# An affine LN with its residual and the plain LN behind it, run as one block chunk by chunk

## The chip, the core and the metric

The kernel runs on one core of a Trainium2 chip. The metric is the time of one execution on the device in microseconds (us): 1481.65 us, the median of three runs (1480.32 to 1482.69).

## The reference

Eight stages A to H work on an activation x of 4 x 1024 tokens by 128 features in float32. Most of them are x + f(LN(x)). The change touches what stands between stage B or D (a feedforward with nine paths, of which each token takes one) and the attention of stage C or E:

```python
def _layernorm(h, gamma, beta):                      # end of the feedforward, EPS = 1e-05
    mu = jnp.mean(h, axis=-1, keepdims=True)
    var = jnp.var(h, axis=-1, keepdims=True)
    return (h - mu) * jax.lax.rsqrt(var + EPS) * gamma + beta
...
    return _layernorm(x + collapsed, gamma, beta)    # added to the residual stream
...
def _layernorm(x, axis=-1, eps=1e-05):               # in front of the next stage, no gain, no bias
    m = jnp.mean(x, axis=axis, keepdims=True)
    v = jnp.var(x, axis=axis, keepdims=True)
    return (x - m) / jnp.sqrt(v + eps)
```

So per place X becomes X + (z - mean) / sqrt(var + eps) * gamma + beta, and Y becomes the plain LN of that new X.

## The kernel before

The activation lies transposed in SBUF: 128 features on the partitions, 4096 tokens (NT) along the free axis. It is worked on in 8 chunks (NCH) of 512 tokens (CH). X is the residual stream, Y what the next stage reads, `k.big[1]` (a part of `arena`) the feedforward's result z. PSUM has eight banks of 128 x 512 float32, `k.bank[0]` to `k.bank[7]`.

The statistics run over the partitions, so TensorE makes them with two constant matrices: `k.center` (identity less 1/128) gives the centered chunk, and `k.mean` (all 1/128) times its squares gives the variance, already spread over all partitions. A float32 matmul of 512 columns shows as two records (and two weight loads) in the trace.

`layernorm` (line 75) is one block: a function for each engine, all of which meet at the block's start and end. It takes the chunks in two loop turns of four (W = 4). For chunk c:
- TensorE (L91) centers it into bank c as soon as `ln_out` says that chunk c - 4 is done, later (L94) makes the variance in bank 4 + c.
- ScalarE squares the centered chunk into `ln_sq` (L103), then makes 1/sqrt(var + eps) as exp(-0.5 ln(var + eps)) in `ln_std`: Ln at L111, Exp at L113.
- VectorE multiplies the two (L122). With gain and bias it applies them in place (L126), and adds the result to X (L130).

Each engine executes its instructions in the order of the code, and each `wait_ge` holds back all that stands behind it on that engine. `ln_out` starts at 4 (`PRIMED`), so that the first four chunks needn't wait.

`stage_ffn` (L806) calls `layernorm` for its input, then `feedforward`, then `layernorm` with gamma, beta and the residual (L811). `stage_favor` and `stage_segments` begin with a block that sets their semaphores (`begin_stage`), then call the plain `layernorm` into Y (L1445, L1785), with the stage's weight loads on SyncE and its small constants on GpSimd in the same block (`favor_loads`, `segment_loads`). After that comes the attention's own block. The stages before and after them, and all other LNs, are the same in both kernels.

Of the kernel before, what the change touches and what calls it, by code (L numbers as in the profile page):

```python
# [6 lines left out]
ALU = mybir.AluOpType  # L7
ACT = mybir.ActivationFunctionType
# [7 lines left out]
CH = 512  # L16
NCH = NT // CH
# [47 lines left out]
def plain(buf, it, c):  # L65

    return buf[:, bass.ds(it * (W * CH) + c * CH, CH)]
# [7 lines left out]
def layernorm(nc, k, call, src, dst, gain=None, bias=None, residual=None, ahead=None):  # L75
# [57 lines left out]
        k.ln_scaled_0 += NCH  # L133
    if residual is not None:
        k.ln_biased_0 += NCH


def rwkv_loads(k, a, block):
# [667 lines left out]
def stage_ffn(nc, k, a, X, Y):  # L806
    call = k.ff_calls
    k.ff_calls += 1
    k.ln(X, lambda it, c: padded(k.N, it, c), ahead=(lambda block: ffn_loads(k, a, block)) if call == 0 else None)
    feedforward(nc, k, a, call)  # L810
    k.ln(lambda it, c: plain(k.big[1], it, c), None, gain="gamma", bias="beta", residual=X)  # L811


def lru(nc, k, a):
# [621 lines left out]
def stage_favor(nc, k, a, X, Y):  # L1436
    with ExitStack() as ctx:
        sems = begin_stage(nc, ctx, FAVOR_SEMS)
        (k.fw_in, k.fw_mask, k.fw_turned, k.fw_wide, k.fw_copied, k.fv_proj, k.fv_sq, k.fv_norm, k.fv_nm, k.fv_v, k.fv_va,
         k.fv_score, k.fv_max, k.fv_off, k.fv_arg, k.fv_exp, k.fv_used, k.fv_ysum, k.fv_acc, k.fv_sums, k.fv_kv,  # L1440
         k.fv_exT, k.fv_ratio, k.fv_ln, k.fv_rd, k.fv_o, k.fv_out, k.fv_x) = sems
        k.ln(X, Y, ahead=lambda block: favor_loads(nc, k, a, block))
        favor(nc, k, a)
        end_stage(nc, sems)

# [334 lines left out]
def stage_segments(nc, k, a, X, Y):  # L1780
    with ExitStack() as ctx:
        sems = begin_stage(nc, ctx, SEGMENT_SEMS)
        (k.sw_in, k.sw_mask, k.sg_proj, k.sg_first, k.sg_kv, k.sg_q, k.sg_kd, k.sg_vd, k.sg_score, k.sg_max, k.sg_arg, k.sg_exp,
         k.sg_sum, k.sg_weight, k.sg_mul, k.sg_turned, k.sg_pT, k.sg_vT, k.sg_vt, k.sg_pv, k.sg_ov, k.sg_out, k.sg_x, k.sg_quarters, k.sg_ln, k.sg_half) = sems
        k.ln(X, Y, ahead=lambda block: segment_loads(nc, k, a, block))  # L1785
        segments(nc, k, a)
        end_stage(nc, sems)

# [1 line left out]

SEMS = ["passed", "ident_zero", "ident_one", "consts_set", "vrows_set", "vecs_in", "vecs_turned", "vecs_ready",
        "x_turned", "x_ready", "x_ready_a", "ln_centered", "ln_squared", "ln_var", "ln_logs", "ln_rstd",
        "ln_scaled", "ln_biased", "ln_out", "y_turned", "y_rows", "y_rows_a", "stored", "wA_in", "moe_w_in", 
        "ff_w_in", "ff_const", "ff_spread", "ff_spread16", "ff_hot0", "ff_mix1", "ff_mix2", "ff_mix", "ff_up",
        "ff_u", "ff_h", "ff_hid", "ff_score", "ff_step", "ff_hot", "ff_hotT", "ff_hot16", "ff_spreads", "ff_masked", "ff_out",
        "ff_z", "lr_w_in", "lr_prod", "lr_read", "lr_init", "lr_sc", "lr_den", "lr_ln", "lr_rden", "lr_step", "lr_x", "lr_kv", "lr_out", "lr_added", "tw_in",
# [13 lines left out]
PRIMED = {"ln_out": 4, "rt_copied": 4,  # L1810
          "ex_r": 4, "ex_relu": 2, "ex_v": 2, "ex_gate": 2, "ex_added": 2, "ex_tanh": 1, "ex_weighed": 1, "ex_sq": 1,
          "ff_h": 6, "ff_out": 1, "ff_hid": 3, "ff_masked": 6, "ff_z": 2, "lr_read": 6, "lr_added": 2,
          "tr_th": 2, "tr_lpT": 1, "tr_x": 2, "tr_z": 2, "tr_g": 1, "tr_turned": 2, "tr_out": 2}
# [122 lines left out]
def build(nc, a, out):  # L1936
    with ExitStack() as ctx:
        def sb(name, shape, dt=F32):
            return ctx.enter_context(nc.sbuf_tensor(name, shape, dt))

        k = Chip()
        k.sems = [ctx.enter_context(nc.semaphore(name)) for name in SEMS]
        (k.passed, k.ident_zero, k.ident_one, k.consts_set, k.vrows_set, k.vecs_in, k.vecs_turned,
         k.vecs_ready, k.x_turned, k.x_ready, k.x_ready_a, k.ln_centered, k.ln_squared, k.ln_var,
         k.ln_logs, k.ln_rstd, k.ln_scaled, k.ln_biased, k.ln_out, k.y_turned, k.y_rows, k.y_rows_a, k.stored, k.wA_in, k.moe_w_in,
         k.ff_w_in, k.ff_const, k.ff_spread, k.ff_spread16, k.ff_hot0, k.ff_mix1,
         k.ff_mix2, k.ff_mix, k.ff_up, k.ff_u, k.ff_h, k.ff_hid, k.ff_score, k.ff_step, k.ff_hot, k.ff_hotT,
         k.ff_hot16, k.ff_spreads, k.ff_masked, k.ff_out, k.ff_z, k.lr_w_in, k.lr_prod, k.lr_read, k.lr_init, k.lr_sc,
# [13 lines left out]
        k.arena = sb("arena", [P, 5 * NT])  # L1962
        k.big = [k.arena[:, i * NT:(i + 1) * NT] for i in range(5)]
        k.rows = k.big[0].rearrange("p (t d) -> p t d", d=P)
        k.ln_calls = k.ff_calls = k.tr_calls = 0

        k.weights = sb("weights", [P, 5120])
        k.eWk = k.weights[:, 0:2048].rearrange("p (e f) -> p e f", e=E)
# [87 lines left out]
```

## Time and profile before

| | us |
|---|---|
| median of three runs | 1481.65 |
| lowest, highest | 1480.32, 1482.69 |
| the profiled execution | 1488.51 |
| its span, first to last instruction | 1486.8 |

The mean granted clock of TensorE in the profiled execution is 0.923 of full speed. All rows come from this one execution; its span is 5 us over the median of the timed runs. Times in the timeline are us from the start of the span. A row of the timeline can merge several instructions of one line; the bracket gives the idle time of the engine before it and what ended it. In the view by stretches the columns are the stretch, its length, the busy us of PE (matmuls), PEld (weight loads), DVE (VectorE), ACT (ScalarE) and POOL (GpSimd) with the count of instructions that start in it, the granted clock of TensorE as a share of full speed, and the DMA share and GB/s.

### The profile page before, as it was taken

What the parts mean: (1) busy time and instruction counts of PE and PEld (TensorE: products, weight loads), DVE (VectorE), ACT (ScalarE), POOL (GpSimd) and SP (SyncE); (2) the same over time, 40 slices, a digit from 0 to 9 for tenths busy, and PEclk for the clock granted to TensorE, in tenths of its full rate; (3) what the DMA queues carried; (4) which work ended last, traced back from release to release, by engine and by line L of the source; (5) the groups of instructions that cost most, each with busy time, mean ns of one, the idle gap of its engine ahead of it and who ended that gap; (6) DMA issues with size and microseconds to landing.
All of it is one profiled execution on the core that took longest, in us unless ns stands there. A gap on an engine that the chain in (4) does not pass through costs nothing. (4 is left out here: it accounts for less than half of the span.)

```text
span 1486.8 us, 22417 instructions
## 1 busy us (share of the span) xinstructions
PE 1226.7 (83%) x7613; PEld 664.2 (45%) x7636; DVE 1006.7 (68%) x1607; ACT 849.1 (57%) x1375; POOL 342.9 (23%) x383
## 2 busy tenths in 40 slices
PE   6888589999999689789997796798898875774656
PEld 3333244444444234257763342376666743431244
DVE  2577458888888355457772555599899945839576
ACT  5677455555555533555675435688877755363442
POOL 0000113333333100000000000187777640005100
PEclk8899889999999889979998999899999998897789
DMA  4000000000000000000000000000000000000001
GB/s 135 1 0 0 0 1 0 0 0 0 0 0 0 9 1 0 8 1 2 2 2 1 0 0 7 1 2 2 2 2 2 3 12 0 0 8 0 0 1 56
DMA packets 9270, 9.77 MB, mean 7 GB/s; under 512 B 2702, under 2 KB 7648, under 8 KB 9184
## 3 DMA queue, kind: packets, MB, share of 16 engines
q1 hardware_dynamic: 9136, 8.61, 1.9%
q8 instruction: 54, 0.88, 0.2%
q14 instruction: 32, 0.26, 0.1%
q10 hardware_dynamic: 48, 0.01, 0.0%
HBM read 6.52 MB, written 2.10 MB: 6 GB/s over the span
## 5 line engine op out<-in xcount | busy, mean ns | idle before, releaser
L575 POOL TENSOR_TENSOR arena<-arena 128x512 f32<-128x512 f32 x64 | 104.7, 1635 | 218.8 <-DVE arena L492 218.8
L556 ACT ACTIVATE arena<-psum 128x512 f32<-128x512 f32 x128 | 69.5, 595 | 127.7 <-PE psum L523 127.7
L523 PE MATMUL psum<-arena,weights 128*128 128x512 f32 x256 | 122.0, 599 | 6.6 <-DVE arena L482 5.9
L538 PE MATMUL psum<-arena,weights 128*128 128x512 f32 x256 | 120.4, 592 | 0.1
L91 PE MATMUL psum<-X,center 128*128 x128 | 75.7, 712 | 35.8 <-PEq L58 16.2
L482 DVE SCALAR_TENSOR_TENSOR arena<-diff,vecs,N 128x512 f32<-128x512 f32 x64 | 102.5, 1602 | 0.0
L122 DVE TENSOR_TENSOR Y<-psum,ln_std 128x512 f32 x48 | 33.2, 692 | 87.9 <-ACT ln_std L113 87.9
L94 PE MATMUL psum<-ln_sq,mean 128*128 128x512 f32 x192 | 91.0, 596 | 0.0
L1656 ACT ACTIVATE N<-N 128x1024 f32<-128x1024 f32 x64 | 67.8, 1059 | 37.5 <-DVE N L1745 36.8
L1562 PE MATMUL psum<-arena 32*128 32x128 f32 x1024 | 79.7, 297 | 4.8 <-ACT arena L1626 4.8
L1572 PE MATMUL psum<-ident,N 128*128 128x128 f32 x512 | 73.2, 288 | 12.3 <-POOL N L1709 11.1
L1562 PEld LDWEIGHTS psum<-arena 32*128 32x128 f32 x1024 | 67.0, 199 | 31.9 <-issue 16.1
L1652 ACT ACTIVATE arena<-psum 128x1024 f32<-128x1024 f32 x64 | 65.5, 1023 | 19.7 <-PE psum L1572 19.5
L489 DVE SCALAR_TENSOR_TENSOR arena<-arena,psum 128x512 f32<-128x512 f32 x64 | 44.0, 687 | 48.3 <-PE psum L538 48.3
L523 PEld LDWEIGHTS psum<-arena,weights 128*128 128x128 f32 x256 | 48.3, 191 | 62.7 <-issue 48.6
L538 PEld LDWEIGHTS psum<-arena,weights 128*128 128x128 f32 x256 | 48.6, 190 | 61.3 <-issue 60.8
L103 ACT ACTIVATE ln_sq<-psum 128x512 f32<-128x512 f32 x96 | 55.0, 589 | 30.0 <-PE psum L91 30.0
L111 ACT ACTIVATE ln_std<-psum,eps 128x512 f32<-128x512 f32 x96 | 64.9, 676 | 7.3 <-PE psum L94 7.3
L563 ACT ACTIVATE arena<-arena 128x1024 f32<-128x1024 f32 x64 | 68.3, 1068 | 0.0
L1709 POOL TENSOR_TENSOR N<-N,arena 128x512 f32<-128x512 f32 x64 | 67.7, 1058 | 0.0
L1708 POOL TENSOR_TENSOR N<-N,arena 128x512 f32<-128x512 f32 x64 | 66.8, 1043 | 2.0 <-ACT arena L1662 2.0
L1572 PEld LDWEIGHTS psum<-ident,N 128*128 128x128 f32 x512 | 57.5, 145 | 21.6 <-POOL N L1709 16.2
(338 smaller groups left out, 2723.8 us busy)
## 6 DMA issues: line engine op xcount, KB each, us to landing
arena<-in_L_attn_a_x_dram SPq DMA_DIRECT2D x4, 512.0 KB, 5.4
out_dram<-arena SPq DMA_DIRECT2D x4, 512.0 KB, 3.3
weights<-in_L_attn_a_eWk_dram SPq DMA_DIRECT2D x1, 1024.0 KB, 5.7
weights<-in_L_attn_a_eWr_dram SPq DMA_DIRECT2D x1, 512.0 KB, 9.4
weights<-in_L_attn_b_W_rkv_dram SPq DMA_DIRECT2D x1, 192.0 KB, 2.3
ffw<-in_L_ffn_W_dram SPq DMA_DIRECT2D x9, 16.0 KB
ffw<-in_L_ffn_W_dram SPq DMA_DIRECT2D x1, 144.0 KB
arena<-n_L_ffn_leaf_values_dram SPq DMA_DIRECT2D x1, 128.0 KB
```

The source lines that it names most:

```text
L91: nc.tensor.matmul(k.bank[c][:], k.center[:], src(it, c), start=True, stop=True).then_inc(k.ln_centered, 1)
L94: nc.tensor.matmul(k.bank[2 + c][:], k.mean[:], k.ln_sq[:, c - 2, :], start=True, stop=True).then_inc(k.ln_var, 1)
L482: nc.vector.scalar_tensor_tensor(mixed[:, j % 4, 1, :], k.diff[:, c, :], k.vec(f"cm_r{e}"), before, ALU.mult, ALU.add).then_inc(k.ex_mix, 1)
L523: op = nc.tensor.matmul(k.bank[2 * (j % 2) + h][:], k.eWk[:, e, h * P:(h + 1) * P], mixed[:, j % 4, 0, :], start=True, stop=True)
L538: op = nc.tensor.matmul(k.bank[4 + j % 2][:], k.eWv[:, e, h, :], ks[:, (2 * (j % 2) + h) * CH:(2 * (j % 2) + h + 1) * CH], start=(h == 0), ...
L556: op = nc.scalar.activation(kr[:, h * CH:(h + 1) * CH], k.bank[2 * (j % 2) + h][:], ACT.Relu)
L563: nc.scalar.activation(ks[:, (j % 2) * 2 * CH:(j % 2 + 1) * 2 * CH], kr, ACT.Square).then_inc(k.ex_sq, 1)
L575: nc.gpsimd.tensor_tensor(acc[:, c, :], acc[:, c, :], oj, ALU.add).then_inc(k.ex_added, 1)
L1562: op = nc.tensor.matmul(scored[half][:, e * P:(e + 1) * P], k.sg_Q[b % 2][at, seg, 2 * j:2 * j + 2, :].rearrange("p h n -> p (h n)"), k.sg ...
L1572: op = nc.tensor.transpose(turned_to[:, e * P:(e + 1) * P], pr[n % 4][:, e * P:(e + 1) * P], k.ident[:])
L1656: nc.scalar.activation(pr[n % 4], pr[n % 4], ACT.Exp).then_inc(k.sg_exp, 1)
L1709: nc.gpsimd.tensor_tensor(others, others, spread(sm[n % 4][:, 8:40]), ALU.mult).then_inc(k.sg_mul, 1)
```

## The change

Both calls, the affine LN at the end of stages B and D and the plain LN at the start of C and E, are replaced by one call of `layernorm_pair` behind `begin_stage`. It takes eight chunks without a loop. Banks 0 and 1 hold the centered chunks of the first LN, 2 and 3 its variances, 4 and 5 the centered chunks of the second, 6 and 7 its variances; the slots of `ln_sq` and `ln_std` are divided in the same way, so that each of these has two places, used by chunks in turn. The first LN has seven semaphores of its own (`lp_...`). In its turn i an engine works on chunk i, i - 1, i - 3 or i - 4, by the step:

```diff
+def layernorm_pair(nc, k, src, gain, bias, dst, ahead):
+
+
+
+    a0, b0 = k.lp_calls * NCH, k.ln_calls * NCH
+    out0 = b0 + PRIMED["ln_out"]
+    first, second = [k.bank[0], k.bank[1]], [k.bank[4], k.bank[5]]
+    first_var, second_var = [k.bank[2], k.bank[3]], [k.bank[6], k.bank[7]]
+    sq = [[k.ln_sq[:, 2 * j + s, :] for s in range(2)] for j in range(2)]
+    std = [[k.ln_std[:, 2 * j + s, :] for s in range(2)] for j in range(2)]
+    scaled = [k.diff[:, s, :] for s in range(2)]
+    at = lambda c: slice(c * CH, (c + 1) * CH)
+    with nc.Block() as block:
+        ahead(block)
+
+        @block.tensor
+        def _(pe):
+            def center(c):
+                if c >= 2:
+                    pe.wait_ge(k.lp_scaled, a0 + c - 1)
+                nc.tensor.matmul(first[c % 2][:], k.center[:], src[:, at(c)], start=True, stop=True).then_inc(k.lp_centered, 1)
+
+            def variance(c):
+                pe.wait_ge(k.lp_squared, a0 + c + 1)
+                if c >= 2:
+                    pe.wait_ge(k.lp_logs, a0 + c - 1)
+                nc.tensor.matmul(first_var[c % 2][:], k.mean[:], sq[0][c % 2], start=True, stop=True).then_inc(k.lp_var, 1)
+
+            def center_again(c):
+                pe.wait_ge(k.lp_out, a0 + c + 1)
+                if c >= 2:
+                    pe.wait_ge(k.ln_out, out0 + c - 1)
+                nc.tensor.matmul(second[c % 2][:], k.center[:], k.X[:, at(c)], start=True, stop=True).then_inc(k.ln_centered, 1)
+
+            def variance_again(c):
+                pe.wait_ge(k.ln_squared, b0 + c + 1)
+                if c >= 2:
+                    pe.wait_ge(k.ln_logs, b0 + c - 1)
+                nc.tensor.matmul(second_var[c % 2][:], k.mean[:], sq[1][c % 2], start=True, stop=True).then_inc(k.ln_var, 1)
+
+            for i in range(NCH + 4):
+                if i < NCH:
+                    center(i)
+                if 0 <= i - 3 < NCH:
+                    center_again(i - 3)
+                if 0 <= i - 1 < NCH:
+                    variance(i - 1)
+                if 0 <= i - 4 < NCH:
+                    variance_again(i - 4)
+
+        @block.scalar
+        def _(act):
+            act.preload_act_table_set("natural_log_exp_and_others")
+
+            def square(c):
+                act.wait_ge(k.lp_centered, a0 + c + 1)
+                if c >= 2:
+                    act.wait_ge(k.lp_var, a0 + c - 1)
+                nc.scalar.activation(sq[0][c % 2], first[c % 2][:], ACT.Square).then_inc(k.lp_squared, 1)
+
+            def over(c):
+                act.wait_ge(k.lp_var, a0 + c + 1)
+                if c >= 2:
+                    act.wait_ge(k.lp_scaled, a0 + c - 1)
+                nc.scalar.activation(std[0][c % 2], first_var[c % 2][:], ACT.Ln, bias=k.eps[:, 0:1]).then_inc(k.lp_logs, 1)
+                act.wait_ge(k.lp_logs, a0 + c + 1)
+                nc.scalar.activation(std[0][c % 2], std[0][c % 2], ACT.Exp, scale=-0.5).then_inc(k.lp_rstd, 1)
+
+            def over_again(c):
+                act.wait_ge(k.ln_var, b0 + c + 1)
+                if c >= 2:
+                    act.wait_ge(k.ln_out, out0 + c - 1)
+                nc.scalar.activation(std[1][c % 2], second_var[c % 2][:], ACT.Ln, bias=k.eps[:, 0:1]).then_inc(k.ln_logs, 1)
+                act.wait_ge(k.ln_logs, b0 + c + 1)
+                nc.scalar.activation(std[1][c % 2], std[1][c % 2], ACT.Exp, scale=-0.5).then_inc(k.ln_rstd, 1)
+
+            for i in range(NCH + 5):
+                if i < NCH:
+                    square(i)
+                if 0 <= i - 4 < NCH:
+                    over_again(i - 4)
+                if 0 <= i - 1 < NCH:
+                    over(i - 1)
+
+        @block.vector
+        def _(dve):
+            def add(c):
+                dve.wait_ge(k.lp_rstd, a0 + c + 1)
+                nc.vector.scalar_tensor_tensor(scaled[c % 2], first[c % 2][:], k.vec(gain), std[0][c % 2], ALU.mult, ALU.mult).then_inc(k.lp_scaled, 1)
+                dve.wait_ge(k.lp_scaled, a0 + c + 1)
+                nc.vector.scalar_tensor_tensor(k.X[:, at(c)], scaled[c % 2], k.vec(bias), k.X[:, at(c)], ALU.add, ALU.add).then_inc(k.lp_out, 1)
+
+            def moment_again(c):
+                dve.wait_ge(k.ln_centered, b0 + c + 1)
+                if c >= 2:
+                    dve.wait_ge(k.ln_var, b0 + c - 1)
+                nc.vector.tensor_tensor(sq[1][c % 2], second[c % 2][:], k.X[:, at(c)], ALU.mult).then_inc(k.ln_squared, 1)
+
+            def scale_again(c):
+                dve.wait_ge(k.ln_rstd, b0 + c + 1)
+                nc.vector.tensor_tensor(dst[:, at(c)], second[c % 2][:], std[1][c % 2], ALU.mult).then_inc(k.ln_out, 1)
+
+            for i in range(NCH + 5):
+                if 0 <= i - 3 < NCH:
+                    moment_again(i - 3)
+                if 0 <= i - 1 < NCH:
+                    add(i - 1)
+                if 0 <= i - 4 < NCH:
+                    scale_again(i - 4)
...
-    k.ln(lambda it, c: plain(k.big[1], it, c), None, gain="gamma", bias="beta", residual=X)
...
-        k.ln(X, Y, ahead=lambda block: favor_loads(nc, k, a, block))
+        layernorm_pair(nc, k, k.big[1], "gamma", "beta", k.Y, lambda block: favor_loads(nc, k, a, block))
...
-        k.ln(X, Y, ahead=lambda block: segment_loads(nc, k, a, block))
+        layernorm_pair(nc, k, k.big[1], "gamma", "beta", k.Y, lambda block: segment_loads(nc, k, a, block))
```

The gain, the bias and the residual of the first LN are now two fused instructions on VectorE (`add`) where there were three. The second moment of the second LN is VectorE's product of the centered chunk with X (`moment_again`), whose mean over the features is the same variance; before, ScalarE squared the centered chunk.

The order of TensorE before, at the end of stage B, from the third chunk of a loop turn on (the first two stand ahead in the same way): each matmul that centers has a wait for `ln_out` ahead of it, and the last variances stand together.

```order
L91 ISA [waits ln_out]
L91 MATMUL psum<-arena,center 128x512
L94 MATMUL psum<-ln_sq,mean 128x512 [waits ln_squared]
L90 REGISTER_ALU
L91 ISA [waits ln_out]
L91 MATMUL psum<-arena,center 128x512
L94 MATMUL psum<-ln_sq,mean 128x512 [waits ln_squared] x3
```

The order of TensorE after, from the fourth chunk on. L158 centers chunk i for the first LN, L170 chunk i - 3 for the second, L164 and L176 make the variances of chunks i - 1 and i - 4.

```order
L158 MATMUL psum<-arena,center 128x512 [waits lp_scaled]
L170 MATMUL psum<-X,center 128x512 [waits lp_out]
L164 MATMUL psum<-ln_sq,mean 128x512 [waits lp_logs,lp_squared]
L176 MATMUL psum<-ln_sq,mean 128x512 [waits ln_squared]
L158 MATMUL psum<-arena,center 128x512 [waits lp_scaled]
L170 MATMUL psum<-X,center 128x512 [waits ln_out,lp_out]
L164 MATMUL psum<-ln_sq,mean 128x512 [waits lp_logs,lp_squared]
L176 MATMUL psum<-ln_sq,mean 128x512 [waits ln_squared]
```

Where before one wait per chunk stood ahead of the matmul and looked four chunks back, now each of the four matmuls of a turn has waits of its own, and `lp_scaled` and `ln_out` look two chunks back.

The order of ScalarE after, the same turns: L196 is the Square of the first LN, L202 and L204 its Ln and Exp, L210 and L212 Ln and Exp of the second.

```order
L196 ACTIVATE ln_sq<-psum 128x512 [waits lp_var,lp_centered]
L210 ACTIVATE ln_std<-psum,eps 128x512 [waits ln_var]
L212 ACTIVATE ln_std<-ln_std 128x512 [waits ln_logs]
L202 ACTIVATE ln_std<-psum,eps 128x512 [waits lp_scaled,lp_var]
L204 ACTIVATE ln_std<-ln_std 128x512 [waits lp_logs]
L196 ACTIVATE ln_sq<-psum 128x512 [waits lp_var,lp_centered]
```

In each turn the Ln and Exp of the second LN (chunk i - 4) stand ahead of those of the first (chunk i - 1).

The order of VectorE after: L226 scales a chunk of the first LN, L228 adds it to X, L234 is the second moment and L238 the final output.

```order
L238 TENSOR_TENSOR Y<-psum,ln_std 128x512 [waits ln_rstd]
L234 TENSOR_TENSOR ln_sq<-psum,X 128x512 [waits ln_var,ln_centered]
L226 SCALAR_TENSOR_TENSOR diff<-psum,vecs,ln_std 128x512 [waits lp_rstd]
L228 SCALAR_TENSOR_TENSOR X<-diff,vecs,X 128x512 [waits lp_scaled]
L238 TENSOR_TENSOR Y<-psum,ln_std 128x512 [waits ln_rstd]
L234 TENSOR_TENSOR ln_sq<-psum,X 128x512 [waits ln_var,ln_centered]
```

The final output of chunk i - 4 stands behind the two instructions for chunk i - 1, and the scaling, the first of these, waits for ScalarE's Exp.

## Rows read from the trace of the kernel before

**Rows 1.** Section 1 of the page: each engine's busy us, share of span, instructions.
```profile
PE 1226.7 (83%) x7613; PEld 664.2 (45%) x7636; DVE 1006.7 (68%) x1607; ACT 849.1 (57%) x1375; POOL 342.9 (23%) x383
```

**Rows 2.** Timeline of both places: start, length, engine, line, operation, count, [idle before].
```profile
599.07 0.69 DVE L693 TENSOR_TENSOR arena<-N,psum 128x512 f32<-128x512 f32 x1 [1.74 <-PE psum L756]
...
600.45 2.84 PE L91 MATMUL psum<-arena,center 128*128 x6 [1.42 <-PEq L628]
...
622.72 0.69 DVE L130 TENSOR_TENSOR X<-X,ln_sq 128x512 f32 x1
...
624.44 4.81 PE L91 MATMUL psum<-X,center 128*128 x6 [6.88 <-PEq L47]
...
643.13 0.69 DVE L122 TENSOR_TENSOR Y<-psum,ln_std 128x512 f32 x1 [0.54 <-ACT ln_std L113]
...
644.14 0.63 PE L1181 MATMUL psum<-ident,arena 128*128 128x128 f32 x4 [3.30 <-PEq L80]
...
899.29 0.69 DVE L693 TENSOR_TENSOR arena<-N,psum 128x512 f32<-128x512 f32 x1 [1.74 <-PE psum L756]
...
944.45 5.39 PE L1538 MATMUL psum<-Y,weights 128*128 128x512 f32 x12 [3.30 <-PEq L80]
```

**Rows 3.** Timeline of steps inside the two LNs of the first place.
```profile
601.61 0.60 ACT L103 ACTIVATE ln_sq<-psum 128x512 f32<-128x512 f32 x1 [0.28 <-PE psum L91]
...
603.12 1.02 PE L94 MATMUL psum<-ln_sq,mean 128*128 128x512 f32 x2
...
603.98 1.02 PE L91 MATMUL psum<-arena,center 128*128 x2
...
604.18 0.69 ACT L111 ACTIVATE ln_std<-psum,eps 128x512 f32<-128x512 f32 x1 [0.26 <-PE psum L94]
...
604.90 0.63 ACT L113 ACTIVATE ln_std<-ln_std 128x512 f32<-128x512 f32 x1
...
605.56 0.69 DVE L122 TENSOR_TENSOR ln_sq<-psum,ln_std 128x512 f32<-128x512 f32 x1 [5.81 <-ACT ln_std L113]
...
606.63 0.63 ACT L113 ACTIVATE ln_std<-ln_std 128x512 f32<-128x512 f32 x1
606.98 0.69 DVE L130 TENSOR_TENSOR X<-X,ln_sq 128x512 f32 x1
607.16 0.67 ACT L111 ACTIVATE ln_std<-psum,eps 128x512 f32<-128x512 f32 x1
607.59 0.68 DVE L122 TENSOR_TENSOR ln_sq<-psum,ln_std 128x512 f32<-128x512 f32 x1
...
607.83 1.12 PE L91 MATMUL psum<-arena,center 128*128 x2 [0.25 <-DVE X L130]
...
626.54 0.60 ACT L103 ACTIVATE ln_sq<-psum 128x512 f32<-128x512 f32 x1 [1.20 <-PE psum L91]
```

**Rows 4.** Groups of VectorE by form: busy us and mean ns behind the bar.
```profile
L482 DVE SCALAR_TENSOR_TENSOR arena<-diff,vecs,N 128x512 f32<-128x512 f32 x64 | 102.5, 1602 | 0.0
...
L661 DVE SCALAR_TENSOR_TENSOR arena<-N,vecs,arena 128x512 f32<-128x512 f32 x16 | 12.0, 751 | 1.5 <-DVE arena L659 0.2
...
L1392 DVE SCALAR_TENSOR_TENSOR X<-psum,vecs,X 128x512 f32<-128x512 f32 x8 | 6.0, 746 | 4.6 <-PE psum L1281 4.6
```

**Rows 5.** Busy time in stretches, three around 88 us and one at 624 us.
```profile
85.00:88.00 3.00, 0.00 (x0) 0.00 (x0) 3.00 (x2) 2.97 (x4) 0.00 (x0) 1.00 0.00 0
...
90.00:92.00 2.00, 2.00 (x4) 0.88 (x3) 1.97 (x2) 0.60 (x1) 0.00 (x0) 0.50 0.00 0
...
94.00:96.00 2.00, 2.00 (x6) 0.83 (x5) 1.97 (x3) 0.85 (x2) 0.00 (x0) 1.00 0.00 0
...
624.00:626.00 2.00, 1.56 (x2) 0.83 (x3) 0.00 (x0) 1.28 (x1) 1.45 (x11) 0.50 0.22 66
```

**Rows 6.** Timeline of TensorE around the last matmuls of that slow stretch.
```profile
88.22 1.22 PE L180 MATMUL psum<-N,mixed 128*128 128x512 f32 x2 [3.32 <-ACT arena L233]
...
93.46 1.02 PE L180 MATMUL psum<-N,mixed 128*128 128x512 f32 x2
```

More of the change, by code:

```diff
@@ L135, in layernorm @@
         k.ln_biased_0 += NCH
+def layernorm_pair(nc, k, src, gain, bias, dst, ahead):
[90 more added lines that the diff above has]
+                    scale_again(i - 4)
+    k.lp_calls += 1
+    k.ln_calls += 1
@@ L1792 @@
         "x_turned", "x_ready", "x_ready_a", "ln_centered", "ln_squared", "ln_var", "ln_logs", "ln_rstd",
-        "ln_scaled", "ln_biased", "ln_out", "y_turned", "y_rows", "y_rows_a", "stored", "wA_in", "moe_w_in",
+        "ln_scaled", "ln_biased", "ln_out", "lp_centered", "lp_squared", "lp_var", "lp_logs", "lp_rstd", "lp_scaled", "lp_out", "y_turned", "y_rows", "y_rows_a", "stored", "wA_in", "moe_w_in",
         "ff_w_in", "ff_const", "ff_spread", "ff_spread16", "ff_hot0", "ff_mix1", "ff_mix2", "ff_mix", "ff_up",
@@ L1944, in build @@
          k.vecs_ready, k.x_turned, k.x_ready, k.x_ready_a, k.ln_centered, k.ln_squared, k.ln_var,
-         k.ln_logs, k.ln_rstd, k.ln_scaled, k.ln_biased, k.ln_out, k.y_turned, k.y_rows, k.y_rows_a, k.stored, k.wA_in, k.moe_w_in,
+         k.ln_logs, k.ln_rstd, k.ln_scaled, k.ln_biased, k.ln_out, k.lp_centered, k.lp_squared, k.lp_var, k.lp_logs, k.lp_rstd, k.lp_scaled, k.lp_out, k.y_turned, k.y_rows, k.y_rows_a, k.stored, k.wA_in, k.moe_w_in,
          k.ff_w_in, k.ff_const, k.ff_spread, k.ff_spread16, k.ff_hot0, k.ff_mix1,
@@ L1964, in build @@
         k.rows = k.big[0].rearrange("p (t d) -> p t d", d=P)
-        k.ln_calls = k.ff_calls = k.tr_calls = 0
+        k.ln_calls = k.lp_calls = k.ff_calls = k.tr_calls = 0
         k.weights = sb("weights", [P, 5120])
```

## The prediction

> **What bounds the kernel now.** The page's busy line first [rows 1]: TensorE is busy for 83% of the span, but that is an average over eight stages, so it says nothing of the two stretches that the change touches. I went from there to the timeline at the two places where an affine LN is followed by a plain one. The last VectorE instruction of the feedforward ends at 599.07 + 0.69 = 599.76, and the next stage's first matmul starts at 644.14 [rows 2]: 44.4 us for both LNs. At the second place it is 899.98 to 944.45, 44.5 us [rows 2]. Between the two LNs lies a join of the engines: 623.41 to 624.44, 1.0 us. TensorE stood still for 6.88 us around it, and its clock was at half when it went on [rows 2, 5]: the first three matmuls of the plain LN take 4.81 us where the affine LN's took 2.84. So the join and the slow start look cheap to save. What the page doesn't show is how closely the merged loop ties the engines to each other, and for that I timed the steps from one engine to the next [rows 3].
>
> **Step times** (full clock, from [rows 3]; the start at 600.45 is in [rows 2]):
> - matmul to the next matmul: 603.98 - 603.12 = 0.86. Matmul to the ScalarE or VectorE instruction that waits for it: 604.18 - 603.12 = 1.06; where the matmul itself had waited, 601.61 - 600.45 = 1.16.
> - Ln to its Exp 604.90 - 604.18 = 0.72; Exp to the next Ln 607.16 - 606.63 = 0.53; Exp to the waiting VectorE instruction 605.56 - 604.90 = 0.66.
> - VectorE to the waiting matmul: 607.83 - 606.98 = 0.85, that is 0.16 behind its end. A VectorE instruction of 0.69 is followed by an independent one after 0.61. Square to matmul: 0.60 + 0.16 = 0.76.
> - The two fused instructions of the new add don't occur in this LN. The nearest rows take 746 ns with PSUM and 751 ns with SBUF alone [rows 4]; so 0.75, followed by an independent one after 0.67. The other end is 1602 ns, the same form in the stage of the experts, where GpSimd has work [rows 4]; for the SBUF one it would add 0.85 to each of five full turns, 8.5 us in all. In the LN GpSimd is busy for 1.45 us at its start [rows 5] and done with it, so I keep 0.75.
>
> **What is removed.** One join of 1.0 us out of two, since the begin of the stage (with its own join) now comes before the pair; a table load; the affine LN's separate scale and shift (0.69 + 0.55 + 0.69 on VectorE become 0.75 + 0.75). What stays at both ends is 1.03 us before the pair and 643.82 to 644.14, 0.32 us, behind it. The moved DMAs and GpSimd's memsets still start with the block and have the whole pair as cover: the pair will be longer than the plain LN that hid them. They cost nothing.
>
> **What is added: a ring.** Before, an LN had four PSUM banks for the centered chunks, so four matmuls ran ahead. Now each of the two has two. `center(i+1)` waits for the scaling of chunk i-1 and `center_again(i-2)` for the final output of chunk i-4, both done by VectorE in its turn i. In that turn VectorE first waits for the Exp of chunk i-1, ScalarE makes it only after `over_again(i-4)`, and that needs `variance_again(i-4)`, the last matmul of TensorE's turn i. So no turn can begin before the one before it has gone through all three engines. Queued behind each waiting matmul on TensorE are all the others of the turn. A full turn, from `center_again` to `center_again`:
> 2 x 0.86 (two matmuls) + 1.06 + Ln 0.72, Exp 0.53, Ln 0.72, Exp 0.66 + 0.75 + 0.67 + 0.85 = 7.68 us per chunk, in which TensorE works for 3.4.
>
> **The pair at full clock**, along this chain:
> - chunk 0 alone: 1.16 + 0.76 + 1.16 + 0.72 + 0.66 + (0.75 + 0.16) = 5.4, then `center(2)`
> - next turn (center, variance): 0.86 + 1.06 + 0.72 + 0.66 + 0.91 = 4.2; the one after it with one matmul more, 5.1: at 14.7
> - first turn with `over_again`, up to `center_again(2)`: 3 x 0.86 + 1.06 + 0.72 + 0.53 + 0.72 + 0.66 + 0.75 + 0.67 + 0.85 = 8.5: at 23.2
> - four turns of 7.68: at 53.9; one with the second LN alone, 0.86 + 1.06 + 0.72 + 0.66 + 0.85 = 4.15: at 58.1
> - end: 1.16 + 0.85 + 1.16 + 0.72 + 0.66 + 0.69 = 5.2. Sum 63.3 us.
>
> **The clock.** In full turns TensorE is idle for 3.6 us before a `center`, and for 4.9 where no `center` is left (1.06 + 0.72 + 0.53 + 0.72 + 0.66 + 0.75 + 0.67 + 0.85, less the matmul's own 1.02); before the last `center_again` about 3.0. The nearest stretch ends at 88.22 us: after 3.32 us without a matmul the granted clock goes from 1.00 to 0.50 (2.4 to 1.2 GHz), the next four matmuls of our shape need 5.24 us (88.22 to 93.46) instead of 4 x 0.86, and then it is back at 1.00 [rows 5, 6]. That is 1.8 us for one gap. The other end is a turn wholly at 1.2 GHz: 3 matmuls at 0.94 more each (the Square behind a slow matmul comes 626.54 - 624.44 = 2.10 after it, not 1.16 [rows 2, 3]), 2.8. I take 2.4 for each of the six gaps and 0.6 for each of the three turns at the start, where TensorE idles 2.3 us: 16 us. Pair: 79 us.
>
> Here the Trainium skill speaks against the change: TensorE: Matmul & The Clock Gate, section "A second HAM failure mode: psum-queue depth-cycling", has the engine idling between groups of matmuls that cycle through PSUM banks and its clock going to and fro between the two levels. The rows at 85 to 93 us agree. Did the rule not hold here, the pair would be the 63.3 us above and the kernel 1522 us; with it, the forecast's 1554.
>
> **Sum.** Each place: 1.03 + 79 + 0.32 = 80.4 against 44.4 (44.5), +36.0; two places +72. On the profiled execution's span of 1486.8 (execution 1488.5) that gives 1559; on the median of 1481.65, which is 5 us under its own profiled span, 1554.
>
> **Rivals.**
> 1. *The clock holds at 2.4 GHz.* For it: from 944.45 us, after a gap of 3.30, twelve matmul records take only 5.39 us [rows 2]. Against it: the slow stretch at 88 us and the slow start at 624.44. Each place 1.03 + 63.3 + 0.32 = 64.7, +20.2; total **1522**.
> 2. *The clock stays at 1.2 GHz through the pair.* 27 matmuls lie on the chain, each 0.94 longer: 63.3 + 25.4 = 88.7, each place +45.6; total **1573**. Against it: at 93 us it is up again after four matmuls [rows 5, 6], and a turn has three or four.
> 3. *The other side: the engines do overlap.* Then the bound is TensorE, 32 matmuls x 0.86 = 27.4, with 8 us of lead and tail: 36.8 with the joins, -7.6 each, total **1466**. It needs the ring loose enough that a full turn costs less than about 5.2 us in place of 7.68 (43 us for the pair is break even). Against it: the terms of a turn are measured one by one, and every one is needed for the next. ScalarE (8 x 3.0) and VectorE (8 x 2.6) would allow it, so only the order of the waits speaks.
> 4. *A partly loose ring*, a step or two off the chain: 1490 to 1520.
>
> **How the numbers follow.** Forecast 0.80, rival 1 0.05, rival 2 0.06, rival 3 0.03, rival 4 0.06. Range: with 1.8 us a gap at the low end the pair is 74 and the total 1544, with 2 us less in the ring 1536; falls that come late in a turn instead of at its start move it to 1530; high, near rival 2, 1572. A measurement tells 0.2% (3 us) from no change; all but rival 3 is slower: faster 0.03, same 0.01, slower 0.96.
>
> **What would show it.** TensorE's longest waits in the pair would be on VectorE's scaling and final output, 3 to 5 us each, about one per chunk; the lines of `center_again` would stand 7.6 to 10 us apart; the granted clock would change up and down in the pair; VectorE and ScalarE would be under half busy there. If `center_again` comes every 3.5 us, the ring is wrong; if every 7.7 at clock 1.00, the clock term is.

## The result, and the profile after

The changed kernel takes 1557.97 us, the median of four runs (1556.48 to 1561.39), against 1481.03 us of the kernel before beside it: ratio 1.05, 95% interval 1.0473 to 1.0527. It is slower by 77 us; the forecast was 1554, with a range of 1530 to 1572. Here and below a ratio and its interval use fast runs alone (runs over 1.5% above the fastest of the same kernel are left out, 1 of 10 in e4 and 3 of 12 in its repetition), while a median is of all runs.

From its page, the span, the busy line and the granted clock in 40 slices:

```profile
span 1559.7 us, 22209 instructions
...
PE 1261.3 (81%) x7613; PEld 677.1 (43%) x7636; DVE 1011.0 (65%) x1607; ACT 839.7 (54%) x1357; POOL 342.8 (22%) x383
...
PEclk9999799999998999669998998679999897898788
```

TensorE has as many instructions as before and 35 us more of busy time [rows 1 for before]: the same matmuls at a slower clock. ScalarE has less work than before, and all engines a smaller share of a longer span.

The ends of the two places, from the timeline, as in [rows 2] (L806 is the feedforward's last add, L158 the pair's first matmul, L238 its last output, L1293 and L1650 the next stages' first matmuls):

```profile
597.11 0.69 DVE L806 TENSOR_TENSOR arena<-N,psum 128x512 f32<-128x512 f32 x1 [1.74 <-PE psum L869]
...
598.45 1.96 PE L158 MATMUL psum<-arena,center 128*128 128x512 f32 x4 [1.38 <-PEq L47]
...
675.43 0.69 DVE L238 TENSOR_TENSOR Y<-psum,ln_std 128x512 f32<-128x512 f32 x1 [1.01 <-ACT ln_std L212]
...
676.44 0.63 PE L1293 MATMUL psum<-ident,arena 128*128 128x128 f32 x4 [2.43 <-PEq L150]
...
931.45 0.69 DVE L806 TENSOR_TENSOR arena<-N,psum 128x512 f32<-128x512 f32 x1 [1.74 <-PE psum L869]
...
1010.96 2.63 PE L1650 MATMUL psum<-Y,weights 128*128 128x512 f32 x4 [2.43 <-PEq L150]
```

The first place is 597.80 to 676.44, 78.64 us where it was 44.4; the second 932.14 to 1010.96, 78.82 where it was 44.5. Together +68.6 us. One full turn, from `center_again` of one chunk to that of the next (L164 and L176 are the variances, L210 and L212 Ln and Exp of the second LN, L202 and L204 those of the first, L226 and L228 the add):

```profile
642.75 1.91 PE L170 MATMUL psum<-X,center 128*128 128x512 f32 x2
...
644.46 1.91 PE L164 MATMUL psum<-ln_sq,mean 128*128 128x512 f32 x2
...
646.16 1.39 PE L176 MATMUL psum<-ln_sq,mean 128*128 128x512 f32 x2
...
647.59 0.69 ACT L210 ACTIVATE ln_std<-psum,eps 128x512 f32<-128x512 f32 x1 [4.00 <-PE psum L176]
648.31 0.63 ACT L212 ACTIVATE ln_std<-ln_std 128x512 f32<-128x512 f32 x1
648.84 0.67 ACT L202 ACTIVATE ln_std<-psum,eps 128x512 f32<-128x512 f32 x1
649.54 0.63 ACT L204 ACTIVATE ln_std<-ln_std 128x512 f32<-128x512 f32 x1
650.21 0.75 DVE L226 SCALAR_TENSOR_TENSOR diff<-psum,vecs,ln_std 128x512 f32<-128x512 f32 x1 [4.81 <-ACT ln_std L204]
650.99 0.75 DVE L228 SCALAR_TENSOR_TENSOR X<-diff,vecs,X 128x512 f32<-128x512 f32 x1
651.66 0.68 DVE L238 TENSOR_TENSOR Y<-psum,ln_std 128x512 f32<-128x512 f32 x1
...
652.49 2.05 PE L170 MATMUL psum<-X,center 128*128 128x512 f32 x2 [4.94 <-DVE Y L238]
```

Read it downwards: three matmuls one behind the other, then both pairs of Ln and Exp, then three VectorE instructions, then the next `center_again`, which ends 4.94 us of idle TensorE. The steps on ScalarE and VectorE, 647.59 to 652.49, take 4.90 us, exactly what the prediction's terms for them add up to. The matmuls ahead of them, 642.75 to 647.59, take 4.84 us where 2.78 was summed at full clock; all that the turn is longer lies there. From the last matmul of the turn to the next turn's first no two engines of this chain work at once. The `center_again` of the first full turn and the two last ones:

```profile
622.89 1.95 PE L170 MATMUL psum<-X,center 128*128 128x512 f32 x2 [0.35 <-DVE Y L238]
...
662.54 2.05 PE L170 MATMUL psum<-X,center 128*128 128x512 f32 x2 [4.94 <-DVE Y L238]
...
668.55 2.04 PE L170 MATMUL psum<-X,center 128*128 128x512 f32 x2 [2.25 <-DVE Y L238]
```

Who waits for whom in the first pair (total us, times, longest):

```profile
DVE diff L226 <- ACT ln_std L204: 32.8, 8, 5.1
ACT ln_std L210 <- PE psum L176: 32.7, 8, 7.5
...
PE psum L158 <- DVE diff L226: 17.1, 6, 3.5
...
PE psum L170 <- DVE Y L238: 12.5, 4, 4.9
```

Each engine waits for the one before it in the ring: ScalarE and VectorE once per chunk, TensorE ten times, on the scaling (L226) or on the final output (L238). The stretches of the pair (columns as in [rows 5]: TensorE's busy time first, the granted clock third from the end):

```profile
598.00:612.00 14.00, 9.10 (x16) 2.97 (x16) 3.69 (x5) 6.30 (x9) 1.45 (x11) 0.90 0.08 20
612.00:640.00 28.00, 15.92 (x25) 5.84 (x24) 7.78 (x11) 10.63 (x17) 0.00 (x0) 0.80 0.00 0
640.00:676.00 36.00, 20.99 (x24) 7.31 (x24) 11.03 (x16) 9.63 (x16) 0.00 (x0) 0.62 0.00 0
```

The mean granted clock is 0.90 in the short turns, 0.80 where the full turns begin and 0.62 in the later ones.

### The profile page after: what moved, and what is told of

Its sections match the earlier page's. It is cut to its first block and busy times, and to the rows that moved or that the text cites. A ratio compares the mean times of both kernels' runs of the same rounds, so it can differ in the third digit from the quotient of the medians.

```text
span 1559.7 us, 22209 instructions
## 1 busy us (share of the span) xinstructions
PE 1261.3 (81%) x7613; PEld 677.1 (43%) x7636; DVE 1011.0 (65%) x1607; ACT 839.7 (54%) x1357; POOL 342.8 (22%) x383
## 5 line engine op out<-in xcount | busy, mean ns | idle before, releaser
L636 PE MATMUL psum<-arena,weights 128*128 128x512 f32 x256 | 122.0, 599 | 6.6 <-DVE arena L595 5.9
L651 PE MATMUL psum<-arena,weights 128*128 128x512 f32 x256 | 120.4, 593 | 0.1
L91 PE MATMUL psum<-X,center 128*128 x96 | 56.0, 703 | 22.0 <-PEq L58 16.3
L639 PE MATMUL psum<-arena,weights 128*128 128x512 f32 x128 | 66.3, 600 | 0.0
L1135 PE MATMUL psum<-arena,weights 128*128 128x512 f32 x64 | 38.2, 727 | 32.1 <-ACT arena L1165 32.1
L1847 DVE TENSOR_REDUCE arena<-psum 128x8 f32<-128x512 f32 x64 | 44.0, 687 | 29.0 <-PE psum L1674 28.8
L840 PE MATMUL psum<-arena,ffw 128*128 128x512 f32 x96 | 50.5, 636 | 14.9 <-DVE arena L776 14.9
```

The source lines that it names most:

```text
L636: op = nc.tensor.matmul(k.bank[2 * (j % 2) + h][:], k.eWk[:, e, h * P:(h + 1) * P], mixed[:, j % 4, 0, :], start=True, stop=True)
L639: nc.tensor.matmul(k.bank[6][:], k.eWr[:, e, :], mixed[:, j % 4, 1, :], start=True, stop=True).then_inc(k.ex_r, 1)
L651: op = nc.tensor.matmul(k.bank[4 + j % 2][:], k.eWv[:, e, h, :], ks[:, (2 * (j % 2) + h) * CH:(2 * (j % 2) + h + 1) * CH], start=(h == 0), ...
```

## The experiments

In every kernel I read the two places in the same rows of the timeline as above, and the time between the places and behind the second.

| kernel | median, us | first place | second place | between them | behind the second |
|---|---|---|---|---|---|
| before | 1481.0 | 44.4 | 44.5 | 255.8 | 542.3 |
| after | 1558.0 | 78.6 | 78.8 | 255.7 | 548.7 |
| e1, first LN ahead on ScalarE | 1523.6 | 61.8 | 58.9 | 255.0 | 548.6 |
| e2, gaps filled | 1541.1 | 66.0 | 66.0 | 266.1 | 550.3 |
| e3, Square on ScalarE | 1559.2 | 78.7 | 78.8 | 255.7 | 541.9 |
| e4, new order | 1479.6 | 36.9 | 36.9 | 256.3 | 549.9 |
| e5, e1 and e2 together | 1521.1 | 55.6 | 55.6 | 262.9 | 547.2 |
| e6, parts without the merge | 1489.0 | 42.0 | 43.2 | 262.8 | 538.8 |
| e7, e4 with Square on ScalarE | 1479.0 | 36.9 | 36.9 | 256.3 | 550.0 |
| e4 again | 1483.0 | 36.9 | 36.9 | 256.3 | 550.0 |
| before again | 1483.4 | 44.4 | 44.5 | 255.8 | 538.8 |
| after again | 1557.3 | 78.7 | 78.9 | 259.0 | 542.0 |

The kernel before measured 1481 us beside the changed kernel, 1488 beside e1 to e4 and 1491 beside e5 to e7 and the second e4, so a median is to be read with its ratio; those below are against the runs beside it. The two last rows are single executions. The columns of the places are from one profiled execution of each kernel, which can lie some us off the median.

### e1: the order within ScalarE's turn

```diff
                 if i < NCH:
                     square(i)
-                if 0 <= i - 4 < NCH:
-                    over_again(i - 4)
                 if 0 <= i - 1 < NCH:
                     over(i - 1)
+                if 0 <= i - 4 < NCH:
+                    over_again(i - 4)
```

> Edit: in ScalarE's turn the Ln and Exp of the first LN (chunk i - 1) stand ahead of those of the second (chunk i - 4); nothing else. Theory (ring through the order of ScalarE's turn): the chain to the scaling no longer goes through variance_again and over_again, a full turn loses one matmul (0.86) and at least one Ln and Exp (1.25) of 7.68, and the pair at full clock is about 52.6 us; with a clock that still falls in most gaps about 60 (57 to 63). Each place 61.4 against 44.4, total about 1481 + 34 = 1515 (1508 to 1522). Rival (the two PSUM banks, or VectorE's added instruction, set the pace whatever the order): 1558 as the changed kernel, within 3 us.

Ratio 1.0252 (1.0205 to 1.0298), places 61.8 and 58.9 where 61.4 was expected. The median of 1523.6 is just over the expected 1508 to 1522, but the kernel before was 7 us over its 1481 beside it; 1.0252 of 1481 is 1518. The two places differ by the clock: its mean is 0.86 in the first and 0.91 in the second. Its timeline, from one `center_again` (L170) to the next:

```profile
625.95 1.10 PE L170 MATMUL psum<-X,center 128*128 128x512 f32 x2 [0.35 <-DVE Y L238]
...
627.94 0.69 ACT L202 ACTIVATE ln_std<-psum,eps 128x512 f32<-128x512 f32 x1 [1.71 <-PE psum L164]
...
629.20 0.67 ACT L210 ACTIVATE ln_std<-psum,eps 128x512 f32<-128x512 f32 x1
629.32 0.75 DVE L226 SCALAR_TENSOR_TENSOR diff<-psum,vecs,ln_std 128x512 f32<-128x512 f32 x1 [1.55 <-ACT ln_std L204]
...
631.61 1.10 PE L170 MATMUL psum<-X,center 128*128 128x512 f32 x2 [0.35 <-DVE Y L238]
```

A full turn is 5.66 us, where the expectation's terms give 7.68 less 0.86 and 1.25, 5.57. ScalarE starts the first LN's Ln (L202) in the middle of the turn, the scaling (L226) follows 1.38 us later, and the second LN's Ln (L210) no longer stands ahead of it. Moving two lines gave back 36.8 us of the 68.6 in the places. The rival, that the two banks or VectorE's work set the pace whatever the order, is out.

### e2: matmuls in the gaps

```diff
                 nc.tensor.matmul(second_var[c % 2][:], k.mean[:], sq[1][c % 2], start=True, stop=True).then_inc(k.ln_var, 1)
+                if c < NCH - 1:
+                    if c >= 1:
+                        pe.wait_ge(k.ln_logs, b0 + c)
+                    fill((c + 1) % 2, (3, 3, 3, 4, 4, 2, 2)[c])
+
+            def fill(to, times):
+                for _ in range(times):
+                    nc.tensor.matmul(second_var[to][:], k.mean[:], k.N[:, 0:CH], start=True, stop=True)
...
                     variance(i - 1)
+                if 1 <= i < 4:
+                    fill(0, 2)
```

> Edit: behind each variance_again (and behind variance in the first turns) TensorE makes 2 to 4 matmuls more, 26 in all in each pair, whose result nobody reads, into the variance bank that is free; they wait for nothing new. They keep TensorE busy in the gaps. Theory (ring of 63.3 us at full clock, and some 15 us from the clock): the clock stays at 1.00 in the pair, full turns take 7.7 us, pair 64 to 65, each place +21, total about 1481 + 43 = 1524, faster than the changed kernel with more work. Rival A (the clock costs little, the chain is longer than summed): the added matmuls delay the others or change nothing, 1555 to 1575. Rival B (only the clock made it slow): at or below the kernel before, 1481 or less.

There are 27 added matmuls in a pair, not 26, and from the second `variance_again` on they do wait for something: the Ln of the turn before (`ln_logs`), which the next `variance_again` would wait for anyway. The trace shows no time lost on that wait. Ratio 1.0345 (1.0278 to 1.0412), both places 66.0. Timeline of two `center_again` (L170) and the added matmuls between them (L184):

```profile
620.63 1.10 PE L170 MATMUL psum<-X,center 128*128 128x512 f32 x2 [0.35 <-DVE Y L248]
...
623.28 2.74 PE L184 MATMUL psum<-N,mean 128*128 128x512 f32 x6
...
628.38 1.10 PE L170 MATMUL psum<-X,center 128*128 128x512 f32 x2 [0.35 <-DVE Y L248]
```

and the whole pair:

```profile
598.00:660.00 62.00, 53.19 (x118) 20.92 (x116) 21.93 (x31) 24.67 (x39) 0.93 (x7) 1.00 0.02 5
```

With the granted clock at 1.00 a full turn is 628.38 - 620.63 = 7.75 us, where 7.68 was summed. TensorE does 27 more matmuls and the place is 12.6 us shorter. So the clock costs at least that. It isn't all: 66.0 is still 21.6 over the kernel before, so rival B is out, and rival A too, with a median of 1541. That median is 17 us over the expected 1524, and the kernel before was 7 over its 1481 beside it. The profiled execution, 6 us over its own median, has 10 us more than the kernel before between the places and 8 more behind the second, where this kernel has the same instructions as the others (last section).

### e3: the second moment back on ScalarE

```diff
+            def square_again(c):
+                act.wait_ge(k.ln_centered, b0 + c + 1)
+                if c >= 2:
+                    act.wait_ge(k.ln_var, b0 + c - 1)
+                nc.scalar.activation(sq[1][c % 2], second[c % 2][:], ACT.Square).then_inc(k.ln_squared, 1)
...
+                if 0 <= i - 3 < NCH:
+                    square_again(i - 3)
                 if 0 <= i - 4 < NCH:
                     over_again(i - 4)
...
-                if 0 <= i - 3 < NCH:
-                    moment_again(i - 3)
```

> Edit: the second moment of the second LN goes back to ScalarE as a Square of the centered chunk (chunk i - 3, ahead of over_again in its turn); VectorE's product is gone. Theory (ring): neither stands on the chain, since variance_again uses the moment of the turn before and ScalarE waits in the same place anyway: 1558, within 5 us (the clock's phase). Rival (VectorE's added work is what costs): 8 instructions of 0.69 per place less on VectorE, 11 us faster, 1547. Second rival (ScalarE is the bound, as its three functions per chunk suggest): 8 Squares of 0.60 per place more, 1568.

Ratio 1.0501 (1.0452 to 1.055), places 78.7 and 78.8: no difference from the changed kernel (ratio 1.05), so both rivals, 1547 and 1568, are out. The timeline shows why (L202 is the Square here, L176 the last variance of the turn, L216 the Ln behind it):

```profile
646.91 0.60 ACT L202 ACTIVATE ln_sq<-psum 128x512 f32<-128x512 f32 x1 [1.11 <-PE psum L170]
...
648.37 1.40 PE L176 MATMUL psum<-ln_sq,mean 128*128 128x512 f32 x2
...
649.81 0.69 ACT L216 ACTIVATE ln_std<-psum,eps 128x512 f32<-128x512 f32 x1 [2.30 <-PE psum L176]
```

The Square is made while ScalarE waits for that variance anyway, and 2.30 us of waiting are left behind it. In this order the named feature of the change, the second moment on VectorE, is worth nothing and costs nothing.

### e4: another order of the same instructions

TensorE's lines are shown as they are, the turns of ScalarE and VectorE in short:

```diff
-                if i < NCH:
-                    center(i)
-                if 0 <= i - 3 < NCH:
-                    center_again(i - 3)
                 if 0 <= i - 1 < NCH:
                     variance(i - 1)
-                if 0 <= i - 4 < NCH:
-                    variance_again(i - 4)
+                if i < NCH:
+                    center(i)
+                if 0 <= i - 3 < NCH:
+                    variance_again(i - 3)
+                if 0 <= i - 2 < NCH:
+                    center_again(i - 2)
... ScalarE
+                over(i - 1); square(i); over_again(i - 3)
... VectorE
+                add(i); moment_again(i - 1); scale_again(i - 2)
```

> Edit: same instructions, same waits, same two banks, only the order in each engine's turn: TensorE variance(i-1), center(i), variance_again(i-3), center_again(i-2); ScalarE over(i-1), square(i), over_again(i-3); VectorE add(i), moment_again(i-1), scale_again(i-2). Theory (the order makes the ring): every chunk's chain fits into two turns, TensorE becomes the bound with 4 x 0.86 = 3.43 us per chunk, pair about 36 us with lead and tail, clock at 1.00 throughout, each place 37.4 against 44.4: total about 1481 - 14 = 1467. Rival (two banks can't hold the overlap): a turn stays over 5.2 us and the time over that of the kernel before, 1485 to 1558.

Both places 36.9. Two matmuls that center a chunk (L158), one turn apart:

```profile
610.38 1.02 PE L158 MATMUL psum<-arena,center 128*128 128x512 f32 x2
...
613.81 1.02 PE L158 MATMUL psum<-arena,center 128*128 128x512 f32 x2
```

and groups of its first pair (busy us, mean ns, then idle before them and what ended it):

```profile
L158 PE MATMUL psum<-arena,center 128*128 128x512 f32 x16 | 8.2, 597 | 1.4 <-PEq L47 1.4
...
L226 DVE SCALAR_TENSOR_TENSOR diff<-psum,vecs,ln_std 128x512 f32<-128x512 f32 x8 | 6.0, 751 | 11.0 <-ACT ln_std L204 11.0
...
L202 ACT ACTIVATE ln_std<-psum,eps 128x512 f32<-128x512 f32 x8 | 5.5, 687 | 5.4 <-PE psum L164 5.4
```

A turn is 3.43 us, four matmuls of 0.86, and TensorE hardly waits in it. Same instructions, same waits, same two banks: the ring was a matter of order alone. The places came out 0.5 us under the expected 37.4, but the total did not: 1479.6 where 1467 was expected, ratio 0.9965 (0.9924 to 1.0006), no difference from the kernel before that these runs tell. It was measured again with more runs:

> The kernel of e4 once more with more rounds, to tell its time from that of the kernel before. Theory: both places stay at 36.9, 7.5 us less than before each, and the rest of the kernel differs from execution to execution by some 7 us whatever stands here; the median is 8 to 15 us under the kernel before, ratio 0.990 to 0.995. Rival (the rest gives the gain back each time, since it starts at another phase of the clock): ratio 0.997 to 1.000.

Ratio 0.9923 (0.9894 to 0.9953), as expected. The medians lie 8.2 us (first time) and 7.6 us (second time) under the kernel before's beside them, while the two places alone are 15.1 us shorter; the runs scatter widely, from 1469.6 to 1495.0. So this order is far faster than the changed kernel and a little faster than the kernel before, and a part of its gain is given back elsewhere. The part behind the second place is 549.9 and 550.0 in the two profiled executions, 8 to 11 over the kernel before's 542.3 and 538.8. Its first matmuls show where this begins (L1650 is the same code as L1538 in [rows 2]):

```profile
927.39 8.23 PE L1650 MATMUL psum<-Y,weights 128*128 128x512 f32 x12 [2.43 <-PEq L150]
```

The twelve records take 8.23 us here and 5.39 in the kernel before. Over the 3712 records from there on the mean granted clock is 0.92 here and 0.94 and 0.96 in the two profiled executions of the kernel before.

### e5: both together

Edit: the diff of e1, and that of e2 with two added matmuls behind each `variance_again` but the last.

> Edit: the swap in ScalarE's turn of e1 and TensorE's added matmuls of e2 together (two behind each of the first three variances and two behind each variance_again but the last, 20 in all per pair). Theory (the order costs and the clock costs are separate terms): the pair comes to the full-clock chain of the swapped order, 52.6 plus about 1.3 for the added matmuls, 53.9; each place 55.3, 3.5 to 6.5 under the 58.9 and 61.8 of e1; total about 1481 + 22 = 1503. Rival (the swap already gave the clock back): places as in e1, 59 to 62.

Ratio 1.0187 (1.0157 to 1.0217), both places 55.6 where 55.3 was expected, with the granted clock at 1.00 in the pair. So order and clock are separate terms, and the chain at full clock comes out in both orders. What the clock costs depends on the order: the added matmuls gave back 12.6 us a place in the old order and 6.2 and 3.3 in this one. The total is 18 over the expected 1503; the kernel before was 10 over its 1481 in this comparison, and the profiled execution has 7 us more than the kernel before between the places and 5 more behind the second.

### e6: the other parts without the merge

On the kernel before, in the two blocks (L130's sum and the separate scale and shift go; `moment` is set for the two plain LNs):

```diff
+                    if residual is not None:
+                        nc.vector.scalar_tensor_tensor(k.ln_sq[:, c, :], k.bank[c][:], k.vec(gain), k.ln_std[:, c, :], ALU.mult, ALU.mult).then_inc(k.ln_scaled, 1)
+                        dve.wait_ge(k.ln_scaled, (it * W + k.ln_scaled_0) + (c + 1))
+                        nc.vector.scalar_tensor_tensor(residual(it, c), k.ln_sq[:, c, :], k.vec(bias), residual(it, c), ALU.add, ALU.add).then_inc(k.ln_out, 1)
+                        continue
...
+                def second_moment(c):
+                    dve.wait_ge(k.ln_centered, g + (c + 1))
+                    nc.vector.tensor_tensor(k.ln_sq[:, c, :], k.bank[c][:], src(it, c), ALU.mult).then_inc(k.ln_squared, 1)
```

> Edit, on the kernel before, without the merge: the affine LN's three VectorE instructions become the two fused ones, and the plain LN's Square becomes VectorE's product. Theory: only the merge costs. The first loop turn of the affine LN waits on VectorE's chain of 0.73 + 0.69 + 0.61, with two fused ones 0.79 + 0.67; about 2.5 us less per affine LN; the plain LN is about 0.6 longer, since VectorE then makes two instructions of 0.61 per chunk and the first output still waits for the whole chain. Each place about 42.4 against 44.4, total 1477. Rival (the second moment on VectorE or the fused forms are a part of the loss): places over 44.4, total over 1483.

Places 42.0 and 43.2, 2.4 and 1.3 us under the kernel before; ratio 0.9989 (0.997 to 1.0007), no difference that the measurement tells. The timeline of the first place tells the parts apart: the affine LN lasts 20.75 us (596.75 to 617.50) where it was 23.65, and the plain LN with its join 21.26 (to 638.76) where it was 20.73. So the fused add gains 2.9 us and the second moment on VectorE loses 0.5, near the expected 2.5 and 0.6. Together they are a gain; the loss of the change is in the merge.

### e7: e4 with the Square on ScalarE

Edit: as in e3, but behind `over_again` and for chunk i - 2.

> Edit, on e4: the second moment of the second LN as a Square on ScalarE, behind over_again in its turn (chunk i - 2); VectorE's product is gone. Theory (TensorE is the bound of e4): ScalarE would need 3.0 + 0.5 = 3.6 us per chunk, just over TensorE's 3.43, so the place becomes about 1 us longer than e4's 36.9: 38. Rival (once nothing waits, every instruction that ScalarE gains counts): 8 x 0.53 = 4.3 us longer, 41.

Ratio 0.9921 (0.9896 to 0.9946), both places 36.9, as e4. I expected 38, and the rival's 41 is out too. Its timeline (L202 is the Square of the second LN, L158 centers a chunk of the first):

```profile
613.08 0.58 ACT L202 ACTIVATE ln_sq<-psum 128x512 f32<-128x512 f32 x1
...
613.31 1.02 PE L158 MATMUL psum<-arena,center 128*128 128x512 f32 x2
...
613.56 0.68 ACT L208 ACTIVATE ln_std<-psum,eps 128x512 f32<-128x512 f32 x1
...
616.53 0.58 ACT L202 ACTIVATE ln_sq<-psum 128x512 f32<-128x512 f32 x1
...
616.75 1.02 PE L158 MATMUL psum<-arena,center 128*128 128x512 f32 x2
```

ScalarE's turn is 3.45 us from Square to Square, TensorE's 3.44. My 3.6 for ScalarE was too high: 3.0 and 0.53 are 3.5, and a Ln starts 0.48 us behind a Square (613.08 to 613.56), where 0.53 was taken. Even without the ring the move to VectorE gains nothing here; both engines sit at the same pace.

### The two kernels again

> The kernel before, unchanged, profiled in another execution. Theory (the two places are set by chains of waits, the rest of the kernel by the phase of the clock): both places 44.4 and 44.5 within 0.5 us, and the parts outside them (255.8 between the places, 542.3 behind the second) off by several us. Rival (the parts outside are as fixed as the places, and what differs there between the kernels is an effect of the change): 255.8 and 542.3 within 1 us.

> The changed kernel, unchanged, profiled in another execution. Theory: the full-clock steps are fixed, but where the clock falls within a turn depends on its phase, so the places are 75 to 83 us, not exactly 78.6 and 78.8 again; outside them the same spread as before's. Rival: 78.6, 78.8, 255.7 and 548.7 within 1 us.

The places of before are the same to 0.02 us. Those of after are 78.7 and 78.9, nearer to the first execution than the expected 75 to 83. Outside the places the expectation of several us holds in part: behind the second place the same kernel differs by 3.5 us (before) and 6.8 us (after) between two executions, between the places by nothing (before, 255.8 both times) and by 3.3 us (after).

## Why the prediction was right, by its steps

- **The ring** was right in mechanism and size. A full turn at full clock was summed to 7.68 and is 7.75 in e2; its steps on ScalarE and VectorE take 4.90 in the changed kernel, as summed. e1 and e4 show that the order of the waits makes it, as argued, and not the two banks.
- **The join** was put at 1.03 us in front of the pair; it is 597.80 to 598.45, 0.65. The end was put at 0.32 and is 676.44 - 676.12 = 0.32.
- **The clock** was put at 16 us; the pair lasts 598.45 to 676.12, 77.7 us, so it is 77.7 - 63.3 = 14.4. It lies otherwise than I laid it. `center_again(2)` starts at 622.89, 24.4 us in, where 23.2 was summed at full clock (I had added 1.8 for the start, it was 1.2). The four turns behind it take 9.84, 10.02, 9.74 and 10.05, 2.2 each over 7.68 (2.4 taken). The next takes 6.0 for 4.15. The end takes 7.6 for 5.2: 2.4 us that I hadn't counted; all its matmuls come at half clock too, the last four records in 3.62 us. The idle time before the last `center_again`, which I gave as about 3.0, is 2.25; my own terms give 2.27.
- **Each place** was put at 80.4 and is 78.6 and 78.8; two places +72, measured +68.6. The spans of the four profiled executions differ by 72.9 and 73.9 us in pairs (1559.7 - 1486.8, 1555.6 - 1481.7), the medians by 77. That the total came within 4 us of the forecast is thus partly luck: the places were put 3.4 us too high, and the parts outside them, put at nothing, were 4 to 8 longer.
- **Covers:** the DMAs and memsets that moved into the pair cost nothing, as said: the waits in the pair are for the engines of the ring and not for them. The fused instructions take 0.75 us each, as taken; the end at 1602 ns did not occur.
- **Rivals.** At 1.2 GHz throughout (1573) and at 2.4 GHz throughout (1522) are both out: the stretches above have means of 0.90, 0.80 and 0.62, and 0.50 or 1.00 was needed. Rival 3, engines that overlap, gave 36.8 us for a place; the changed kernel doesn't do it, but e4, with its instructions in another order, takes 36.9. Rival 4, a partly loose ring (1490 to 1520), is out for the changed kernel by the turn of 7.75 us; e1, with a turn of 5.66, is such a ring.
- **Signs.** `center_again` came 9.7 to 10.1 us apart (7.6 to 10 said), TensorE's longest waits on VectorE were 3.5 and 4.9 us, and VectorE and ScalarE were under half busy. The low end of the range has a slip: 2 us less in the ring of each place takes 1544 to 1540, not to 1536. The result doesn't rest on it.
- **What was left open.** The part behind the second place is 550.0 us in e4 and e7 and 542.3 or 538.8 before, so that about half of their gain is gone. The instructions there are the same and the clock is lower; why it is lower was not settled.

## What to carry to other kernels

When two pipelines are merged, write down for one turn which instruction of each engine waits for which of the others: if the last instruction of the first engine's turn is needed by the second engine ahead of what the first engine's next turn needs, the turns can't overlap, however idle each engine looks. Put the instruction that frees the other engines first in each turn, and give each chunk's steps at least one turn of distance; here the same 32 matmuls went from 78.6 to 36.9 us by that alone. An engine's share of busy time says only what is possible; the sum of step times around the ring says what will be.

## What the runs showed of the hardware

The prediction had one row to go by, a gap of 3.32 us. In the changed kernel TensorE's clock also fell with shorter gaps. Early in the changed kernel's first pair, in turns of 4.20 us (603.71 to 607.91) with 2.22 us of idle time each, the matmul behind the gap still runs as at full clock, and the next one doesn't:

```profile
607.91 1.13 PE L158 MATMUL psum<-arena,center 128*128 128x512 f32 x2 [2.22 <-DVE diff L226]
608.88 1.45 PE L170 MATMUL psum<-X,center 128*128 128x512 f32 x2
```

That is 1.45 us instead of 1.02. In the stretch where full turns with a gap of 3.46 us begin, the mean granted clock is 0.80.

What I hadn't expected is how far this reaches into stages that the change doesn't touch. A stretch of the stage behind the first place, 1674 matmul records of the same code, in the kernel before and in e2:

```profile
644.00:804.00 160.00, 144.79 (x1674) 103.49 (x1675) 104.82 (x143) 90.45 (x142) 0.00 (x0) 0.92 0.01 2
```

```profile
662.50:830.00 167.50, 152.66 (x1674) 110.02 (x1675) 104.73 (x143) 90.51 (x142) 0.00 (x0) 0.88 0.01 1
```

It is 7.5 us longer in e2, with 8 us more of TensorE's busy time at a granted clock of 0.88 instead of 0.92. The whole way to the second place takes 255.8 us in one and 266.1 in the other. The stage behind the second place, 3712 records, in e6 and in the changed kernel:

```profile
944.14:1215.20 271.06, 228.11 (x3712) 171.75 (x3712) 233.11 (x401) 202.90 (x373) 193.94 (x224) 0.96 0.01 2
```

```profile
1010.70:1288.60 277.90, 236.04 (x3712) 178.32 (x3712) 233.07 (x400) 202.87 (x373) 193.87 (x224) 0.93 0.01 2
```

271.06 us at 0.96, 277.90 at 0.93. That e2 came out slower than its places say is this effect by these rows. The same is read for e5 and for e6, which has no merge: between the places they take 263 us at a mean clock of 0.91, the kernel before 256 at 0.93. A slow start is not all of it: in e2 and e5 the twelve records behind the second place take 5.39 us as before, and the part behind that place is still 550.3 and 547.2. What decides how a stage's clock will go was not tried. Whoever measures a change of a few us should read the time of the changed stretch itself beside the total.
